# The gate and up products of a ternary feed-forward kernel, turned to a seven-product scheme over half blocks

## The reference

```
h   = gelu(gelu(cond_128 @ W0 + b0) @ W1 + b1);  att = softmax(h @ W2 + b2)         # (64, 8)
y   = einsum('boi,bih->boh', einsum('bk,koi->boi', att, weight), x) + (att @ bias_k)[:, :, None]
bitlinear(v, w): s = mean(|w|); q = round(clip(w / (s + 1e-5), -1, 1)); return v @ (q * s).T
out = x + bitlinear(bitlinear(y, w_gate) * bitlinear(y, w_up), w_down)             # 1024 -> 2752 -> 1024
```

## Time and profile before

| | |
|---|---|
| time, median of 3 runs | 1955.59 us (1955.26 to 1955.91) |
| span of the profiled execution | 1954.9 us |
| PE, DVE, ACT, POOL busy in the span | 97%, 31%, 23%, 7% |
| chunk to chunk, from the fourth on | 231.9 us |

### The profile page before, as it was taken

The page is one execution under the profiler, slowest core; times in us unless marked ns, Lnnn a source line. Parts: engine busy times, 40 slices in busy tenths (PEclk is TensorE's granted clock), DMA queues, the critical chain, the costliest instruction groups (busy, mean ns, idle before and its releaser), DMA issues.

```text
span 1954.9 us, 22867 instructions
## 1 busy us (share of the span) xinstructions
PE 1897.3 (97%) x9127; PEld 897.0 (46%) x9127; DVE 603.1 (31%) x902; ACT 440.8 (23%) x712; POOL 131.6 (7%) x73
## 2 busy tenths in 40 slices
PE   5688999999999999999999999999999999999999
PEld 3344454445444454444544454444544445444444
DVE  6989941024310242103510144102431024200320
ACT  4766530212102120111202122021210212011100
POOL 0864400000000000000000000000000000000000
PEclk8899999999999999999999999999999999999999
DMA  7536210100001000010001000010000100000000
GB/s 283 197 121 237 86 55 32 44 1 1 22 23 43 1 1 27 17 44 1 6 32 50 0 1 17 28 44 1 1 22 23 44 0 1 27 17 1 1 11 33
DMA packets 27744, 77.91 MB, mean 40 GB/s; under 512 B 4160, under 2 KB 4480, under 8 KB 27648
## 3 DMA queue, kind: packets, MB, share of 16 engines
q1 hardware_dynamic: 27648, 76.43, 11.1%
HBM read 59.65 MB, written 16.78 MB: 39 GB/s over the span
## 4 chain that ended last, share of the span: by engine, by line
PE 92%; DVE 3%; issue 2%; ACT 2%; POOL 1%; DMA 0%; SPq 0%; DVEq 0%; ACTq 0%; POOLq 0%
PE ps L435 91%; DVE msk L913 1%; ACT g_r L665 1%; POOL ys L407 1%; DVE msk L905 0%; PE ps L517 0%; DVE aT L226 0%; ACT wgT L694 0%; DMA inter<-in_L_cond_b_dram 0%; POOL ab L418 0%; DVE wsum L784 0%; DVE ys L832 0%; ACT wuT L694 0%; POOL bbc L418 0%; DVE inter L953 0%
## 5 line engine op out<-in xcount | busy, mean ns | idle before, releaser
L435 PE MATMUL ps<-yp,wuT 128*128 128x512 f16 x2688 | 596.4, 380 | 0.0
L435 PE MATMUL ps<-wdT,inter 128*128 128x512 fp8e4 x2688 | 590.6, 379 | 0.0
L435 PE MATMUL ps<-yp,wgT 128*128 128x512 f16 x2688 | 586.6, 380 | 2.2 <-ACT wgT L694 1.1
L435 PEld LDWEIGHTS ps<-wdT,inter 128*128 128x128 f16 x2688 | 263.0, 98 | 316.2
L435 PEld LDWEIGHTS ps<-yp,wgT 128*128 128x128 fp8e4 x2688 | 262.1, 98 | 316.5 <-issue 5.1
L435 PEld LDWEIGHTS ps<-yp,wuT 128*128 128x128 fp8e4 x2688 | 262.3, 98 | 307.5 <-issue 8.3
L725 ACT COPY inter<-ps 128x512 f32<-128x512 f32 x168 | 98.5, 586 | 817.1 <-PE ps L435 817.1
L941 DVE SCALAR_TENSOR_TENSOR prod<-ps,inter 128x512 f32<-128x512 f32 x168 | 116.0, 690 | 328.3 <-PE ps L435 328.3
L739 ACT CAST inter<-prod 128x512 f16<-128x512 f32 x168 | 103.8, 618 | 441.2 <-DVE prod L941 441.2
L962 DVE SCALAR_TENSOR_TENSOR xr<-ps,osc,xr 128x512 f32<-128x512 f32 x64 | 48.0, 750 | 466.5 <-PE ps L435 466.5
L937 DVE SCALAR_TENSOR_TENSOR prod<-ps,g_r 64x512 f32<-64x512 f32 x8 | 5.6, 694 | 522.1 <-ACT g_r L733 522.0
(11 more groups left out here) (143 smaller groups left out, 646.4 us busy)
## 6 DMA issues: line engine op xcount, KB each, us to landing
xa<-in_x_dram SPq DMA_DIRECT2D x8, 2048.0 KB, 7.9
out_dram<-xr SPq DMA_DIRECT2D x64, 256.0 KB, 2.0
wdT<-in_L_ffn_w_up_dram SPq DMA_DIRECT2D x10, 512.0 KB, 4.8
ys<-in_L_ffn_w_down_dram SPq DMA_DIRECT2D x9, 512.0 KB, 4.2
xr<-in_L_ffn_w_down_dram SPq DMA_DIRECT2D x8, 512.0 KB, 4.5
inter<-in_L_ffn_w_gate_dram SPq DMA_DIRECT2D x7, 512.0 KB, 15.6
xr<-in_L_ffn_w_down_dram SPq DMA_DIRECT2D x8, 352.0 KB, 4.5
wdT<-in_L_ffn_w_gate_dram SPq DMA_DIRECT2D x5, 512.0 KB, 5.5
```

What stands on the lines that cost most here:

```text
L435: return nc.tensor.matmul(o, l, r, start=start, stop=stop)
```

## The change

From chunk FIRST = 2 on, gate and up are computed by the Winograd form of Strassen's scheme. A pair of weight tiles b1, b2 (features f and f + 1) and the two halves of the inputs (blocks 0 to 3 and 4 to 7) make a 2x2 block matrix; the two halves of the tokens (256 each) and the same halves of the inputs make another. Seven products of half blocks take the place of eight. Half h = 0 of a pair is gate, h = 1 up, written beside each other into one bank (256 + 256 columns). The 21st gate tile and the 21st up tile form an eleventh pair of half width. The remainder tile stays as it was.

- In chunk 1 DVE forms, for each of 21 pairs of tiles, seven weight blocks (four sums, three copies), and SP stores them to a DRAM scratch `wcomb`. From chunk 2 on SP streams them back, pair by pair, into a ring three pairs deep in the space of wgT.
- y's quarters and four sums of them (`sum_quarter`) are split into hi and lo (`hi_quarters` on ACT, `lo_quarter` on DVE) while the chunk before does its down product.
- PE accumulates P2 onto P1, P7 and P4 onto P6, P3 onto P5; between them ACT copies P1 out (`top`) and DVE adds the sums (`lower`) and multiplies gate by up in four quarters (`inter11` to `inter22`).
- The order of the down product is turned so that the remainder comes second to last; L1_LOG goes from 14 to 13, one bit less in the scale of y.
- Chunk 1 stands unrolled ahead of the loops, and so does chunk 2.

The core of the diff:

```diff
+    HALF = TOK // 2
+    KQ = KH // 2
+    NPR = FT // 2
+    NS = NPR + 1
+    RING = 3
+    BLK = KQ * P
+    PART = 7 * BLK
+    FIRST = 2
+    A11, A21, A12, A22, S1, S2, S3, S4 = range(8)
+    OPERAND = {"P1": A11, "P6": S2, "P5": S1, "P2": A12, "P7": S3, "P4": A22, "P3": S4}
+    BLOCK = {"P1": 0, "P6": 1, "P5": 2, "P2": 3, "P7": 4, "P4": 5, "P3": 6}
...
+        PA, PB, PC = (ps[0], ps[3]), (ps[1], ps[4]), (ps[2], ps[5])
+        WRB, DNC = ps[3], (ps[5], ps[2])
+
+        wcomb = nc.dram_tensor("wcomb", [NS, 2, P, PART // 4], f32).ap()
...
+        def ring(p, h, b, k):
+            at = ((p % RING) * 2 + h) * PART + b * BLK + k * P
+            return wg_flat[:, at:at + P]
+
+        def stage(i):
+            return (raw5[:, :].bitcast(f8), msk_flat)[i % 2][:, 0:PART]
+
+        yp_hl = (yp[:, :, :, :].rearrange("p k i n -> p (k i n)"),
+                 wu_flat[:, 0:4 * KH * TOK].bitcast(f16))
+
+        def operand(i, s):
+            return yp_hl[i].rearrange("p (s k n) -> p s k n", s=8, k=KQ)[:, s, :, :]
...
+        def quarter(s):
+            if s == S1:
+                return prod[:, :, :].rearrange("p a n -> p (a n)").rearrange("p (k n) -> p k n", k=KQ)
+            s = {S2: A11, S3: A21, S4: A12}.get(s, s)
+            k, t = (s // 2) * KQ, (s % 2) * HALF
+            return ys[:, k:k + KQ, t:t + HALF]
+
+        t1 = [raw5[:, i * TOK:(i + 1) * TOK] for i in range(2)]
+        q6 = [msk_flat.bitcast(f32)[:, i * TOK:(i + 1) * TOK] for i in range(2)]
+        rr = [wu_flat[:, 4 * KH * TOK:4 * KH * TOK + 8 * TOK].bitcast(f32)[:, i * TOK:(i + 1) * TOK] for i in range(2)]
+        q67, g11 = g_r, hi_r[:, :].bitcast(f32)
...
+            def ring_load(p):
+                at = (p % RING) * 2 * PART
+                if p < NPR:
+                    dst = wg_flat[:, at:at + 2 * PART].bitcast(f32).rearrange("p (h n) -> p h n", h=2)
+                    sp.dma_start(dst, wcomb[p].rearrange("h p n -> p h n")).then_inc(s_ring[p % RING], 16)
+                else:
+                    sp.dma_start(wg_flat[:, at:at + PART].bitcast(f32), wcomb[p, 0]).then_inc(s_ring[p % RING], 16)
+
+            def next_pairs(c):
+                for p, before in ((0, NPR - 1), (1, NPR), (2, NPR - 2)):
+                    sp.wait_ge(s_m3, NS * (c - FIRST) + before + 1)
+                    ring_load(p)
+
+            def pairs(c, more):
+                for p in range(RING, NS):
+                    sp.wait_ge(s_m3, NS * (c - FIRST) + p - RING + 1)
+                    ring_load(p)
+                    if more and p == 5:
+                        next_x(c)
+
+            next_x(1)
+            for i in range(2 * NPR + 1):
+                sp.wait_ge(s_comb, i + 1)
+                sp.dma_start(wcomb[i // 2, i % 2], stage(i).bitcast(f32)).then_inc(s_wst[i % 2], 16)
+            sp.wait_ge(s_gu, GU + FT)
+            for i in range(2):
+                sp.wait_ge(s_wst[i], 16 * (NPR + 1 - i))
+            for p in range(RING):
+                ring_load(p)
+            store(1)
+
+            def chunk(c):
+                pairs(c, True)
+                next_pairs(c)
                 store(c)
+
+            chunk(FIRST)
+            with sp.Fori(FIRST + 1, NC - 1) as c:
+                chunk(c)
...
+            def product(c, p, what):
+                n = NS * (c - FIRST) + p
+                first, start = isinstance(c, int) and c == FIRST, what in ("P1", "P6", "P5")
+                bank = {"P1": PA, "P2": PA, "P6": PB, "P7": PB, "P4": PB, "P5": PC, "P3": PC}[what][p % 2]
+                if what == "P1":
+                    pe.wait_ge(s_ring[p % RING], 16 * ((4, 4, 3)[p % RING] * (c - FIRST) + p // RING + 1))
+                    if p >= 2:
+                        pe.wait_ge(s_i11, NPR * (c - FIRST) + p - 1)
+                    elif first:
+                        pe.wait_ge(s_uv, UP * FIRST)
+                    elif p == 0:
+                        pe.wait_ge(s_f1, n)
+                    else:
+                        pe.wait_ge(s_uvr, c - FIRST)
+                elif what == "P6":
+                    if p >= 2:
+                        pe.wait_ge(s_c21, n - 1)
+                    elif first and p == 1:
+                        pe.wait_ge(s_o, DN * FIRST)
+                    elif not first:
+                        pe.wait_ge(s_c21, n if p == 0 else n - 1)
+                elif what == "P5":
+                    if p >= 2:
+                        pe.wait_ge(s_c12, n - 1)
+                    else:
+                        pe.wait_ge(s_o, DN * c)
+                elif what == "P2":
+                    pe.wait_ge(s_t1, n + 1)
+                elif what == "P7":
+                    pe.wait_ge(s_q6, n + 1)
+                elif what == "P4":
+                    pe.wait_ge(s_q67, n + 1)
+                elif what == "P3":
+                    pe.wait_ge(s_c22, n + 1)
+                if p == 0:
+                    pe.wait_ge(s_ylo, KH * c + OPERAND[what] + 1)
+                waited(c)
+                for h in range(2 if p < NPR else 1):
+                    out = bank[:, h * HALF:(h + 1) * HALF]
+                    for k in range(KQ):
+                        w = ring(p, h, BLOCK[what], k)
+                        for i in range(2):
+                            last = nc.tensor.matmul(out, w, operand(i, OPERAND[what])[:, k, :],
+                                                    start=(start and h + k + i == 0), stop=(k == KQ - 1 and i == 1),
+                                                    skip_group_check=True)
+                last.then_inc(s_done[what], 1)
+
+            def rest(c):
+
+                pe.wait_ge(s_i11, NPR * (c - FIRST) + NPR)
+                waited(c)
+                for k in range(KH):
+                    for i in range(2):
+                        last = mm(WRB[:, :].rearrange("p (t n) -> p t n", t=2), wrT[:, k, :], both_halves(i, k),
+                                  start=(k + i == 0), stop=(k == KH - 1 and i == 1))
+                last.then_inc(s_wr, 1)
+
...
+            def pairs(c, more):
+                for p in range(NS):
+                    product(c, p, "P1")
+                    product(c, p, "P6")
+                    if p:
+                        product(c, p - 1, "P4")
+                    if more and p - 5 in range(KH // 2):
+                        conv(c + 1, 2 * (p - 5))
+                    product(c, p, "P5")
+                    if p:
+                        product(c, p - 1, "P3")
+                    if more and p - 5 in range(KH // 2):
+                        conv(c + 1, 2 * (p - 5) + 1)
+                    if more and p == 4:
+                        agg_b(c + 1)
+                    product(c, p, "P2")
+                    product(c, p, "P7")
+                rest(c)
+                product(c, NPR, "P4")
+                product(c, NPR, "P3")
+                downs(c, more)
+
+            pairs(FIRST, True)
+            with pe.Fori(FIRST + 1, NC - 1) as c:
...
+            def top(c, p):
+                n, w = NS * (c - FIRST) + p, TOK if p < NPR else HALF
+                act.wait_ge(s_m1, n + 1)
+                if p >= 2:
+                    act.wait_ge(s_c21, n - 1)
+                elif p == 0 and not (isinstance(c, int) and c == FIRST):
+                    act.wait_ge(s_c21, n)
+                nc.scalar.copy(t1[p % 2][:, 0:w], PA[p % 2][:, 0:w]).then_inc(s_t1, 1)
+
+            def gate11(c, p):
+                n = NS * (c - FIRST) + p
+                act.wait_ge(s_m2, n + 1)
+                if p:
+                    act.wait_ge(s_i11, NPR * (c - FIRST) + p)
+                nc.scalar.copy(g11, PA[p % 2][:, 0:HALF]).then_inc(s_g11, 1)
+
+            def hi_first(c, p):
+                act.wait_ge(s_f1, NS * (c - FIRST) + p + 1)
+                nc.scalar.copy(part(2 * p, 0), prod[:, 0, :]).then_inc(s_uhi, 1)
+
+            def hi_second(c, p):
+                act.wait_ge(s_f2, NPR * (c - FIRST) + p + 1)
+                nc.scalar.copy(part(2 * p + 1, 0), prod[:, 1, :]).then_inc(s_uhi, 1)
+
...
+                if more and not (isinstance(c, int) and c + 1 < FIRST):
+                    sum_quarter(c + 1, S1)
+                    lo_quarter(c + 1, A11)
+                    output(c, 1)
+                    lo_quarter(c + 1, A21)
+                    sum_quarter(c + 1, S3)
+                    output(c, 2)
+                    sum_quarter(c + 1, S2)
+                    lo_quarter(c + 1, A12)
+                    output(c, 3)
+                    sum_quarter(c + 1, S4)
+                    lo_quarter(c + 1, A22)
...
+            def combine(i):
+
+                h = i % 2
+                w1, w2 = ((wgT, wgT), (wuT, wuT))[h] if i < 2 * NPR else (wgT, wuT)
+                f = i // 2 * 2
+                g = f + 1 if i < 2 * NPR else f
+                b1, b2 = w1[:, :, f * P:(f + 1) * P], w2[:, :, g * P:(g + 1) * P]
+                st = stage(i).rearrange("p (b k f) -> p b k f", b=7, k=KQ)
+                if i == 0:
```

(159 more changed lines are left out.)

117 lines of the change are left out of this document (109 added, 8 removed).

## The result

| | before | after |
|---|---|---|
| median | 1955.75 us (4 runs, 1955.26 to 1957.69) | 1855.67 us (4 runs, 1854.43 to 1856.45) |
| span of the profiled execution | 1954.9 us | 1853.5 us |
| ratio | | 0.9484, 95% interval 0.947 to 0.9497 |

The forecast was 1856 us. The page after shows PE as busy as before, at the same granted clock, with DVE now at half of the span (it stands beside the earlier trace rows).

What follows compares the result with a forecast made beforehand. PE, busy for 97% of the span at full clock, was taken as the bound. 1955.6 - 100.4 - 1.4 + 1.0 = 1854.8, with a microsecond for semaphore waits 1856 us; range 1848 to 1890.

Steps and rivals of the forecast that it cites:

- The pace: PE's matmuls of 256 columns: 109.1 ns each, 106.7 for the columns plus 2.4, with the weight load hidden.
- rival (a): On PE, weight load or instruction issue does not hide behind 109 ns: 2045 us at 135.9 ns; chance 0.07 below 123 ns, 0.05 above.
- Gate and up: Chunks 2 to 7: gate and up fall from 148.5 to 131.8 us a chunk, 16.7 us less, 100.4 in six.
- The products don't wait: Within a pair PE never waits for DVE or ACT: 2.6 us spare, about 1.7 with convolutions; zero booked.
- The start of a chunk: First products no longer wait for the last output or first split: six times about 0.25 us, 1.4 us gained.
- Transfers: Combined weights streamed from DRAM, 0.92 MB a pair at 75 GB/s, with loads of x between: zero cost.
- The combinations: Weight sums on DVE in chunk 1: 3.5 us each, the first 14 done 4 us before PE stops; 1 us booked.
- rival (b): In chunk 1 SP's order or slow fp8 operations make the combinations late: 5 to 38 us once, 1860 to 1893; chance 0.12.
- rival (c): Products wait for DVE and ACT in every pair; 1.5 us a pair gives no change, 1955; chance 0.04 with a scheme saving nothing.
- semaphore waits: A microsecond added to the sum for a semaphore wait here and there, giving 1856 us.

Runs made afterwards that it cites:

- kernel with eight products: The kernel after with product P5 computed twice in every pair, so eight half-block products stand in a pair: 1968.96 us, ratio to before 1.0064.
- the first experiment: The kernel before with each 512-column gate and up matmul issued as two of 256 or four of 128 columns: 1968.19 and 1994.35 us against 1956.35.
- the third: The kernel after with idle DVE operations ahead of q67 in each pair, delays of 2.2, 2.9 and 4.4 us: 1860.95, 1875.54 and 1976.53 us.

## Why the prediction was right

- **The pace** (109.1 ns, from 55 at 128 and 215.8 at 512 columns): 109.2 in the products, and 109.2 and 55.9 in two kernels made for it. The upper bound taken from the fp32 convolution (111) wasn't needed. The burst of 82.5 ns on which rival (a) rested was a mean: in the trace the first seven of its eight transposes start 56 ns apart (196.67 to 197.01 us), the eighth 149 ns after the seventh, and the next group 176 ns after that.
- **Gate and up** (16.7 us a chunk, 100.4 in six): a chunk went from 231.7 to 214.9, 16.8 us, and the stretch of six by 100.6. The kernel with eight products shows that nothing else in the scheme gains.
- **The products don't wait** (2.6 us spare): shown by the profile for the kernel itself, and by the three delays for the size of the margin. For pairs with convolutions I had put 1.7, 0.9 less than for the others; at 4.4 us of delay PE waits only 0.3 to 0.4 us longer in them, so they have nearly as much. That is a step that was too careful and cost nothing. DVE's load was as put: in the whole pair from 1007.44 to 1019.66 us it is busy for 6.4 of 12.2 us, where 6.5 stood.
- **The start of a chunk** (six times about 0.25 us, 1.4 us gained): not so. The chain before has rows of "issue" at four of the six starts (0.36 us at 569.37, 0.12 at 1033.07, 0.21 at 1264.87, 0.36 at 1496.77, none at the starts of the chunks 3 and 7), 1.05 us in all. After, the three turns reached by a jump back take 0.7 us more than the other chunks. So some 0.3 us were gained. The loss of the old code was probably the jump back of its loop, which runs over the chunks 1 to 6, and not the wait for the last output; I didn't run the old code written out, so this is not shown. The term was sized by a wait that a row of "issue" didn't name.
- **Transfers** (zero): PE has no wait for the ring. The load of x in chunk 1 took 9.0 us, where 7.9 was put, and the median of such loads is now 10.2 us against 7.9; there is slack for it.
- **The combinations** (3.5 us each, 1 us booked, a margin of 4 us): the stall behind SP's load came as forecast, to the microsecond (376.7 against 377). One costs 2.82 us, since all seven operations start 0.6 us apart or less, so the margin was 12 us (411.6 against 424) and nothing was lost. For rival (b) the price was put too low: with combinations twice as long, the clock alone cost 5 us on top of PE's waits, and the bias copy has no slack at all.
- **Rival (a)** is ruled out by the first experiment, **rival (c)** by the profile and the third.

The errors of the small terms cancel in part: of 1.4 us gained only 0.3 came, and of 2 us lost (1 for the combinations, 1 for semaphore waits) none. That the forecast and the result are 0.3 us apart is luck within them.

## What to carry to other kernels

When PE streams without a gap, count its time as columns at the full clock and a fixed 2.5 ns for each matmul (as measured here at 128, 256 and 512 columns), and ask of any scheme that trades columns for more, smaller matmuls whether the product left out is larger than that: here an eighth of the columns against 504 more matmuls a chunk, 17.9 us against 1.2. Then price the margin, not the load, of the engines that now stand between two products: DVE may be at 54% and still hold PE if its work comes 3 us later. A wait of PE can cost more than its length: behind the waits of 22.7 and 6.0 us PE did 4.5 and 5.6 us of its work at half the clock. And count the slack of every dependence by itself, since the bias copy had none where the products had three groups.
